# Small steps of the folded maxima with one operand in PSUM, and five key blocks by keys in the last attention

## The chip, the cores and the metric

The kernel runs on one core of a Trainium2 chip. The metric is device time in microseconds of one execution, median of several runs. TensorE (PE) multiplies matrices into PSUM, VectorE (DVE) and ScalarE (ACT) work on SBUF and PSUM, GpSimd (POOL) works on SBUF, and SyncE (SP) issues the loads and stores.

## What is computed

Two attention layers follow each other, on two images of 1024 positions and 256 channels. Of the reference this matters:

```
xn = group_norm(x, gamma, beta)            # 32 groups
q, k, v = conv1x1(xn, wq, bq), conv1x1(xn, wk, bk), conv1x1(xn, wv, bv)
scores = einsum('bnc,bmc->bnm', q, k) * C ** -0.5
attn = softmax(scores, axis=-1)
out = conv1x1(einsum('bnm,bmc->bnc', attn, v), wp, bp) + x
```

The second layer does the same with its own weights on the output of the first.

## The kernel before

**Units and chunks.** A unit `u` (0 to 3) is one image in one layer: units 0 and 1 are the images in layer one, 2 and 3 in layer two. A unit has 1024 queries, handled as two chunks of 512, so there are eight chunks `c` from 0 to 7; chunk `2u` is called `first` and chunk `2u + 1` `second` in the code. A chunk has eight key blocks `kb` of 128 keys and four query blocks `j` of 128 queries.

**One chunk.** PE makes the scores of a key block, 128 keys by 512 queries, in one of six PSUM banks (`ring`) with six matmuls (L1027 to L1029). ACT copies them to `S` in SBUF (L449), and DVE keeps a running maximum over the key blocks in `R` (L673). When all eight blocks are in, the maximum over the 128 partitions of `R` must be had for each query and stand on all partitions. For chunks 0 and 1 PE does this with transposes. For chunks 2 to 7 DVE does it alone in `maxima_to_all` (L689 to L721): a transpose of 32x32 squares into the PSUM bank `X`, a reduction of `X` to `folded` (128x16), then eight small steps on 64 or 32 partitions and 16 columns that fold the four groups of 32 partitions into one minimum of the negated values, subtract and add the query's own value `w_query`, and write `spread`; a last transpose spreads it over the whole bank `X`. Each of these steps waits for the one before it by the semaphore `dv_fold`. Then DVE adds `X` to each block of `S` (`shifted`, L729), ACT takes the exponential twice (L456 to `P_hi`, L457 back to `S`), and POOL makes `P_lo`, the difference of the two (L312). The attention of a chunk multiplies `P_hi` and `P_lo` with the values `V` (`attend`, L1066 to L1068, three matmuls for a query block and a key block, accumulated in one bank for each query block). DVE divides by the row sum and adds to `xnat` (`output`, L735 and L739), and in layer two SP stores the rows (L279).

**Order.** Every engine's order is written out by hand, and semaphores are counted. On PE the order in a unit is: values of the unit (`values`, L1013 to L1015), scores of `first`, attention of the chunk before, scores of `second`, attention of `first`, and between its second and third query block the product `t` for the next unit's first half. `values` and `scores` use banks of the ring in turn; a bank is free when DVE has read it, so `values(u, 6)` waits for DVE's `v_low(u, 0)` (L662, L664), which itself follows ACT's `v_high(u, 0)` (L442). While DVE does `maxima_to_all(second)` in units 1 and 2, POOL does `x_low` for the next unit, four subtractions of 128x512 in SBUF (L336). In the first score block of the second half PE also transposes rows of `xnat` for the next unit (`next_rows`, L914), which waits for DVE's `output`.

**The end.** The attention of the last chunk has nothing behind it to hide it. Its first four key blocks are multiplied as they come (`attention_by_keys`: for one `kb`, all four query blocks, behind a wait for that block's `P_lo`). Then one wait asks for `P_lo` of all eight blocks, and the other four are done query block by query block (L1162), so that each query block can be divided and stored while the next is multiplied.

The functions that the change touches follow, and what calls them.

Of the kernel before, what the change touches and what calls it, by code (L numbers as in the profile page):

```python
# [7 lines left out]
ALU = mybir.AluOpType  # L8
# [3 lines left out]
P = 128  # L12
# [7 lines left out]
def two_attention_layers(nc, x, layers, vectors, out):  # L20
# [17 lines left out]
    NB = N // P  # L38
# [3 lines left out]
    SQ = 32  # L42
    BLOCKS = BANK // SQ
    QUARTERS = P // SQ
    BY_PE = 2
    W_COPIES = 2 * QUARTERS
    PER_GROUP = C // GROUPS
    WX = C + 2
# [14 lines left out]
    def tile_of(c, kb):  # L63

        return (c * NB + kb) % TILES
# [28 lines left out]
    with ExitStack() as ctx:  # L94
        def sb(name, shape, dt=F32, stack=ctx):
            return stack.enter_context(nc.sbuf_tensor(name, shape, dt))

        def ps(name):
            return ctx.enter_context(nc.psum_tensor(name, [P, BANK], F32))

        def sem(name):
            return ctx.enter_context(nc.semaphore(name))
# [23 lines left out]
        neg_less = sb("neg_less", [P, QB])  # L126
        neg_shift = sb("neg_shift", [P, QB])
        folded = sb("folded", [P, 2, BLOCKS])
        other = sb("other", [2 * SQ, 2, BLOCKS])
        w_query = sb("w_query", [2 * SQ, HALVES, BLOCKS])  # L130
        spread = sb("spread", [P, BLOCKS])
        S = sb("S", [P, TILES, BANK])
# [31 lines left out]
        X = ps("X")  # L164
# [60 lines left out]
        dv_fold = sem("dv_fold")  # L225
        dv_X = sem("dv_X")
# [9 lines left out]
        def count_R(c, kb):  # L236

            return c * (NB - 1) + kb
# [45 lines left out]
        def _(pool):  # L284
# [30 lines left out]
            def values_of_queries(u):  # L315
# [5 lines left out]
                pool.wait_ge(po_resid, (u + 1) * NB)  # L321
                for n in range(W_COPIES):
                    g, to = divmod(n, 2)

                    if n:
                        pool.wait_ge(po_w, (u - 1) * W_COPIES + n)
                    nc.gpsimd.tensor_copy(by_group[to * SQ:(to + 1) * SQ, g],
                                          w_row[g * SQ:(g + 1) * SQ, :].rearrange("p (h j) -> p h j", j=QB)
                                          ).then_inc(po_w, 1)
                pool.wait_ge(po_w, u * W_COPIES)  # L330

# [198 lines left out]
        def _(dve):  # L530
# [158 lines left out]
            def maxima_to_all(c):  # L689

                half, quarter, n = 2 * SQ, SQ, c - BY_PE
                dve.wait_ge(dv_R, count_R(c, NB - 1))
                nc.vector.transpose(X[:], R[:]).then_inc(dv_fold, 1)
                dve.wait_ge(dv_fold, 7 * n + 1)
                nc.vector.tensor_reduce(folded[:, 0, :], X[:, :].rearrange("p (b n) -> p b n", n=SQ), AX_X, ALU.max,
                                        negate=True).then_inc(dv_fold, 1)  # L700
                dve.wait_ge(dv_fold, 7 * n + 2)
                nc.vector.tensor_copy(other[0:half, 0, :], folded[half:P, 0, :]).then_inc(dv_fold, 1)
                dve.wait_ge(dv_fold, 7 * n + 3)
                nc.vector.tensor_tensor(folded[0:half, 1, :], folded[0:half, 0, :], other[0:half, 0, :], ALU.min
                                        ).then_inc(dv_fold, 1)
                dve.wait_ge(dv_fold, 7 * n + 4)
                nc.vector.tensor_copy(other[0:quarter, 1, :], folded[quarter:half, 1, :])
                nc.vector.tensor_copy(other[quarter:half, 1, :], folded[0:quarter, 1, :]).then_inc(dv_fold, 1)
                dve.wait_ge(dv_fold, 7 * n + 5)
                nc.vector.tensor_tensor(other[0:half, 0, :], folded[0:half, 1, :], other[0:half, 1, :], ALU.min  # L710
                                        ).then_inc(dv_fold, 1)

                w = w_query[:, c % 2, :]
                dve.wait_ge(po_w, c // 2 * W_COPIES)
                dve.wait_ge(dv_fold, 7 * n + 6)
                nc.vector.tensor_tensor(folded[0:half, 1, :], other[0:half, 0, :], w, ALU.subtract).then_inc(dv_fold, 1)
                dve.wait_ge(dv_fold, 7 * n + 7)
                nc.vector.tensor_tensor(spread[0:half, :], folded[0:half, 1, :], w, ALU.add)
                nc.vector.tensor_tensor(spread[half:P, :], folded[0:half, 1, :], w, ALU.add).then_inc(dv_X, 1)
                dve.wait_ge(dv_X, 2 * n + 1)  # L720
                nc.vector.transpose(X[:], spread[:, :, None].to_broadcast([P, BLOCKS, SQ])).then_inc(dv_X, 1)  # L721

            def shifted(c, kb):
                if c < BY_PE:
                    dve.wait_ge(pe_M, c + 1)
                else:
                    dve.wait_ge(dv_X, 2 * (c - BY_PE) + 2)
                tile = S[:, tile_of(c, kb), :]
                nc.vector.tensor_tensor(tile, X[:], tile, ALU.add).then_inc(dv_D, 1)  # L729
# [63 lines left out]
            for u in range(1, UNITS):  # L793
# [8 lines left out]
                for kb in range(1, NB):  # L802
                    running_max(first, kb)
                    if more and kb in (3, 6):
                        statistics_of(u + 1, kb // 3 - 1)

                maxima_to_all(first)
                output(before, 0)
                for kb in range(4):
# [32 lines left out]
                running_max(second, 7)  # L842

                maxima_to_all(second)
                output(first, 0)
                shifted(second, 0)
# [24 lines left out]
        def _(pe):  # L871
# [191 lines left out]
            def attend(c, j, kb):  # L1063
                v, tile, mine = V[(c // 2) % 2], exp_of(c, kb), slice(j * P, (j + 1) * P)
                bank = bank_of("O", c, j)
                nc.tensor.matmul(bank[:, 0:C + 2], P_hi[:, tile, mine], v[:, kb, 0:C + 2], start=(kb == 0), stop=False)  # L1066
                nc.tensor.matmul(bank[:, 0:C], P_hi[:, tile, mine], v[:, kb, C + 2:VX], start=False, stop=False)  # L1067
                last = nc.tensor.matmul(bank[:, 0:C + 2], P_lo[:, tile, mine], v[:, kb, 0:C + 2],  # L1068
                                        start=False, stop=(kb == NB - 1))
                if kb == NB - 1:  # L1070
                    last.then_inc(pe_O, 1)
# [13 lines left out]
            def attention_by_keys(c, kb):  # L1085

                pe.wait_ge(po_P, c * NB + kb + 1)
                for j in range(QB):
                    if kb == 0:
                        wait_for_bank("O", c, j)  # L1090
                    attend(c, j, kb)
# [64 lines left out]

                attention(first, next_first_half, lambda: None)

            for kb in range(NB // 2):
                attention_by_keys(CHUNKS - 1, kb)  # L1160
            pe.wait_ge(po_P, CHUNKS * NB)
            for j in range(QB):  # L1162
                for kb in range(NB // 2, NB):
                    attend(CHUNKS - 1, j, kb)


# [30 lines left out]
```

## Time and profile before

| | us |
|---|---|
| median of 3 runs | 264.69 |
| range of the runs | 264.43 to 264.79 |
| the profiled execution, whole | 264.73 |
| its span, first to last instruction | 262.6 |

The busy times in the profiled execution are PE 254.3 us, DVE 187.5, ACT 153.3 and POOL 124.2. The granted TensorE clock is 1.0 in all 40 slices of the span. PE's busy time hides short gaps, since the end of a matmul is modelled: where it matters, read the starts of two neighbouring rows. Matmuls of 256 or 258 columns start 0.12 us apart when nothing holds them, those of 512 columns 0.23 us apart.

### The profile page before, as it was taken

How to read it: one execution, taken by the hardware profiler on the slowest of the kernel's cores; microseconds unless marked ns; L12 is line 12 of the kernel's file. 1: busy time of each engine (PE TensorE's matmuls, PEld its weight loads, DVE VectorE, ACT ScalarE, POOL GpSimd, SP SyncE). 2: the span in 40 equal slices, each digit the busy share in tenths (PEclk: the TensorE clock that was granted, in tenths of full speed). 3: DMA queues.
4: the chain of work that ended last, by engine and by line, in shares of the span. 5: the costliest groups of instructions: out<-in, count | busy, mean ns of one | idle time of the engine just before them, and what ended most of it. 6: DMA issues, size and time to landing. Idle time of an engine off the chain costs nothing.

```text
span 262.6 us, 4590 instructions
## 1 busy us (share of the span) xinstructions
PE 254.3 (97%) x1614; PEld 228.2 (87%) x1614; DVE 187.5 (71%) x473; ACT 153.3 (58%) x299; POOL 124.2 (47%) x143
## 2 busy tenths in 40 slices
PE   7999999999999999999989999999999999999985
PEld 6787789889998899789987899789987899889985
DVE  0589977886983797679776698679776688549703
ACT  3656544699984519645667509746486509740920
POOL 2010801285769209517475907717274917800860
PEclk9999999999999999999999999999999999999999
DMA  6960000000000000000000000000110001100102
GB/s 201 347 217 0 0 1 2 0 0 2 0 4 0 0 2 1 0 2 1 0 1 2 0 2 0 0 2 0 41 41 3 0 2 40 40 2 19 50 14 80
DMA packets 6989, 7.37 MB, mean 28 GB/s; under 512 B 556, under 2 KB 6712, under 8 KB 6968
## 3 DMA queue, kind: packets, MB, share of 16 engines
q1 hardware_dynamic: 6944, 7.08, 8.1%
q8 instruction: 13, 0.21, 0.4%
q14 instruction: 8, 0.07, 0.1%
q10 hardware_dynamic: 24, 0.01, 0.0%
HBM read 4.99 MB, written 2.10 MB: 27 GB/s over the span
## 4 chain that ended last, share of the span: by engine, by line
PE 60%; DVE 21%; ACT 8%; issue 6%; POOL 4%; POOLq 0%; DVEq 0%; ACTq 0%
PE ring L1027 11%; PE ring L1029 10%; PE ring L1028 10%; PE ring L1066 5%; PE ring L1068 4%; PE ring L1067 4%; DVE S L729 4%; POOL P_lo L312 3%; ACT P_hi L456 3%; DVE xnat L739 2%; PE ring L1013 2%; ACT S L457 2%; PE ring L1014 2%; PE ring L1015 2%; PE Z L914 2%
## 5 line engine op out<-in xcount | busy, mean ns | idle before, releaser
L312 POOL TENSOR_TENSOR P_lo<-S,P_hi 128x512 fp32r<-128x512 f32 x64 | 81.9, 1302 | 73.7 <-ACT S L457 73.5
L1066 PE MATMUL ring<-V,P_hi 128*128 128x258 f32 x256 | 72.9, 285 | 0.9 <-POOL P_lo L312 0.9
L1068 PE MATMUL ring<-V,P_lo 128*128 128x258 f32 x256 | 72.2, 282 | 0.0
L1067 PE MATMUL ring<-V,P_hi 128*128 128x256 f32 x256 | 72.2, 282 | 0.0
L456 ACT ACTIVATE P_hi<-S 128x512 fp32r<-128x512 f32 x64 | 40.2, 628 | 43.0 <-DVE S L729 43.0
L449 ACT COPY S<-ring 128x512 f32<-128x512 f32 x64 | 37.2, 589 | 37.9 <-PE ring L1029 36.2
L1027 PE MATMUL ring<-t_hi,xn_lo 128*128 128x512 f32 x128 | 51.8, 405 | 0.0
L1029 PE MATMUL ring<-t_hi,xn_hi 128*128 128x512 f32 x128 | 50.0, 391 | 0.0
L1028 PE MATMUL ring<-t_lo,xn_hi 128*128 128x512 f32 x128 | 50.0, 391 | 0.0
L1066 PEld LDWEIGHTS ring<-V,P_hi 128*128 128x128 f32 x256 | 48.4, 189 | 1.6 <-POOL P_lo L312 1.1
L1067 PEld LDWEIGHTS ring<-V,P_hi 128*128 128x128 f32 x256 | 48.4, 189 | 0.5
L1068 PEld LDWEIGHTS ring<-V,P_lo 128*128 128x128 f32 x256 | 48.6, 190 | 0.0
L673 DVE TENSOR_TENSOR R<-ring,R 128x512 f32<-128x512 f32 x48 | 33.1, 691 | 20.0 <-ACT S L449 19.6
L729 DVE TENSOR_TENSOR S<-X,S 128x512 f32<-128x512 f32 x64 | 41.4, 681 | 1.2 <-PE X L1059 1.2
L457 ACT ACTIVATE S<-S 128x512 f32<-128x512 f32 x64 | 39.8, 622 | 0.0
L308 POOL TENSOR_TENSOR xnat<-xnat,out_bias 128x256 f32<-128x256 f32 x32 | 23.0, 750 | 12.2 <-DVE out_bias L573 12.2
L1027 PEld LDWEIGHTS ring<-t_hi,xn_lo 128*128 128x128 f32 x128 | 24.1, 188 | 5.2 <-issue 0.8
L1029 PEld LDWEIGHTS ring<-t_hi,xn_hi 128*128 128x128 f32 x128 | 24.0, 188 | 5.2
L1028 PEld LDWEIGHTS ring<-t_lo,xn_hi 128*128 128x128 f32 x128 | 24.1, 188 | 4.2
L1013 PE MATMUL ring<-Wx_hi,xn_lo 128*128 128x258 f32 x64 | 18.7, 292 | 1.6 <-DVE w_row L664 1.5
L662 DVE TENSOR_TENSOR V<-ring,V 128x256 fp32r<-128x256 f32 x32 | 13.4, 419 | 9.0 <-ACT V L442 8.9
L1014 PE MATMUL ring<-Wx_lo,xn_hi 128*128 128x258 f32 x64 | 18.2, 284 | 0.0
(116 smaller groups left out, 355.4 us busy)
## 6 DMA issues: line engine op xcount, KB each, us to landing
xnat<-in_x SPq DMA_DIRECT2D x8, 256.0 KB, 6.9
out<-xnat SPq DMA_DIRECT2D x16, 128.0 KB, 1.7
wide<-in_vectors SPq DMA_DIRECT2D x2, 384.0 KB, 7.6
w_wq<-in_L_conv_wq SPq DMA_DIRECT2D x2, 256.0 KB, 4.8
w_wk<-in_L_conv_wk SPq DMA_DIRECT2D x2, 256.0 KB, 5.0
w_wv<-in_L_conv_wv SPq DMA_DIRECT2D x2, 256.0 KB, 6.9
w_wp<-in_L_conv_wp SPq DMA_DIRECT2D x1, 256.0 KB, 6.6
w_wp<-in_L_conv_wo SPq DMA_DIRECT2D x1, 256.0 KB, 7.5
```

What stands on the lines that cost most here:

```text
L312: nc.gpsimd.tensor_tensor(P_lo[:, exp_of(c, kb), :], S[:, tile_of(c, kb), :], P_hi[:, exp_of(c, kb), :].bitcast(F32), ALU.subtract).then_i ...
L449: nc.scalar.copy(S[:, tile_of(c, kb), :], bank_of("S", c, kb)[:]).then_inc(ac_S, 1)
L456: nc.scalar.activation(P_hi[:, exp_of(c, kb), :], S[:, tile, :], ACT.Exp)
L457: nc.scalar.activation(S[:, tile, :], S[:, tile, :], ACT.Exp).then_inc(ac_P, 1)
L673: nc.vector.tensor_tensor(R[:], bank_of("S", c, kb)[:], earlier, ALU.max).then_inc(dv_R, 1)
L729: nc.vector.tensor_tensor(tile, X[:], tile, ALU.add).then_inc(dv_D, 1)
L1027: nc.tensor.matmul(bank[:], xn_lo[:, kc, keys], t_hi[:, kc, cols], start=(kc == 0), stop=False)
L1028: nc.tensor.matmul(bank[:], xn_hi[:, kc, keys], t_lo[:, kc, cols], start=False, stop=False)
L1029: last = nc.tensor.matmul(bank[:], xn_hi[:, kc, keys], t_hi[:, kc, cols], start=False, stop=(kc == KC - 1))
L1066: nc.tensor.matmul(bank[:, 0:C + 2], P_hi[:, tile, mine], v[:, kb, 0:C + 2], start=(kb == 0), stop=False)
L1067: nc.tensor.matmul(bank[:, 0:C], P_hi[:, tile, mine], v[:, kb, C + 2:VX], start=False, stop=False)
L1068: last = nc.tensor.matmul(bank[:, 0:C + 2], P_lo[:, tile, mine], v[:, kb, 0:C + 2], start=False, stop=(kb == NB - 1))
```

## The change

**One.** The buffer `other` in SBUF is gone. The small steps of `maxima_to_all` keep their number, order, sizes and waits, but four groups of 16 columns at the front of the bank `X`, which the reduction before them has finished reading, take the place of `other` and of the second half of `folded` where needed, so that every step has one operand (a source or the destination) in PSUM and none has two sources in SBUF.

**Two.** In the last attention five key blocks instead of four are done by keys, and three instead of four by query block, behind the wait for all `P_lo`.

```diff
+    BY_KEYS = 5
...
-        other = sb("other", [2 * SQ, 2, BLOCKS])
...
-                nc.vector.tensor_copy(other[0:half, 0, :], folded[half:P, 0, :]).then_inc(dv_fold, 1)
+
+                at = [X[:, BLOCKS * m:BLOCKS * (m + 1)] for m in range(4)]
+                nc.vector.tensor_copy(at[0][0:half], folded[half:P, 0, :]).then_inc(dv_fold, 1)
                 dve.wait_ge(dv_fold, 7 * n + 3)
-                nc.vector.tensor_tensor(folded[0:half, 1, :], folded[0:half, 0, :], other[0:half, 0, :], ALU.min
+                nc.vector.tensor_tensor(folded[0:half, 1, :], at[0][0:half], folded[0:half, 0, :], ALU.min
                                         ).then_inc(dv_fold, 1)
                 dve.wait_ge(dv_fold, 7 * n + 4)
-                nc.vector.tensor_copy(other[0:quarter, 1, :], folded[quarter:half, 1, :])
-                nc.vector.tensor_copy(other[quarter:half, 1, :], folded[0:quarter, 1, :]).then_inc(dv_fold, 1)
+                nc.vector.tensor_copy(at[1][0:quarter], folded[quarter:half, 1, :])
+                nc.vector.tensor_copy(at[1][quarter:half], folded[0:quarter, 1, :]).then_inc(dv_fold, 1)
                 dve.wait_ge(dv_fold, 7 * n + 5)
-                nc.vector.tensor_tensor(other[0:half, 0, :], folded[0:half, 1, :], other[0:half, 1, :], ALU.min
+                nc.vector.tensor_tensor(at[2][0:half], at[1][0:half], folded[0:half, 1, :], ALU.min
...
-                nc.vector.tensor_tensor(folded[0:half, 1, :], other[0:half, 0, :], w, ALU.subtract).then_inc(dv_fold, 1)
+                nc.vector.tensor_tensor(at[3][0:half], at[2][0:half], w, ALU.subtract).then_inc(dv_fold, 1)
                 dve.wait_ge(dv_fold, 7 * n + 7)
-                nc.vector.tensor_tensor(spread[0:half, :], folded[0:half, 1, :], w, ALU.add)
-                nc.vector.tensor_tensor(spread[half:P, :], folded[0:half, 1, :], w, ALU.add).then_inc(dv_X, 1)
+                nc.vector.tensor_tensor(spread[0:half, :], at[3][0:half], w, ALU.add)
+                nc.vector.tensor_tensor(spread[half:P, :], at[3][0:half], w, ALU.add).then_inc(dv_X, 1)
...
-            for kb in range(NB // 2):
+            for kb in range(BY_KEYS):
                 attention_by_keys(CHUNKS - 1, kb)
             pe.wait_ge(po_P, CHUNKS * NB)
             for j in range(QB):
-                for kb in range(NB // 2, NB):
+                for kb in range(BY_KEYS, NB):
                     attend(CHUNKS - 1, j, kb)
```

On DVE, in each of the six calls of `maxima_to_all`, this stood in a row before, between the reduction of `X` and the last transpose:

```order
L699 TENSOR_REDUCE folded<-X 128x16 [waits dv_fold]
L702 COPY other<-folded 64x16 [waits dv_fold]
L704 TENSOR_TENSOR folded<-folded,other 64x16 [waits dv_fold]
L707 COPY other<-folded 32x16 [waits dv_fold]
L708 COPY other<-folded 32x16
L710 TENSOR_TENSOR other<-folded,other 64x16 [waits dv_fold]
L716 TENSOR_TENSOR folded<-other,w_query 64x16 [waits dv_fold,po_w]
L718 TENSOR_TENSOR spread<-folded,w_query 64x16 [waits dv_fold]
L719 TENSOR_TENSOR spread<-folded,w_query 64x16
```

At the same place on DVE there stands now:

```order
L699 TENSOR_REDUCE folded<-X 128x16 [waits dv_fold]
L704 COPY X<-folded 64x16 [waits dv_fold]
L706 TENSOR_TENSOR folded<-X,folded 64x16 [waits dv_fold]
L709 COPY X<-folded 32x16 [waits dv_fold]
L710 COPY X<-folded 32x16
L712 TENSOR_TENSOR X<-X,folded 64x16 [waits dv_fold]
L718 TENSOR_TENSOR X<-X,w_query 64x16 [waits dv_fold,po_w]
L720 TENSOR_TENSOR spread<-X,w_query 64x16 [waits dv_fold]
L721 TENSOR_TENSOR spread<-X,w_query 64x16
```

Nothing moved here; only the operands differ, five steps read `X` and five write it.

On PE, in the attention of the last chunk (ring2 to ring5 are the banks of its four query blocks), this stood before around the wait for all of `P_lo`, which is the wait in these rows:

```order
L1068 MATMUL ring5<-V1,P_lo 128x258
L1066 MATMUL ring2<-V1,P_hi 128x258 [waits po_P]
L1067 MATMUL ring2<-V1,P_hi 128x256
L1068 MATMUL ring2<-V1,P_lo 128x258
L1066 MATMUL ring2<-V1,P_hi 128x258
```

At the same place in PE's order this stands now; the first wait is for the fifth block alone, the second for all:

```order
L1070 MATMUL ring5<-V1,P_lo 128x258
L1068 MATMUL ring2<-V1,P_hi 128x258 [waits po_P]
L1069 MATMUL ring2<-V1,P_hi 128x256
L1070 MATMUL ring2<-V1,P_lo 128x258
L1068 MATMUL ring3<-V1,P_hi 128x258
...
L1070 MATMUL ring5<-V1,P_lo 128x258
L1068 MATMUL ring2<-V1,P_hi 128x258 [waits po_P]
```

The wait for all of `P_lo` has moved twelve matmuls later; its former place waits only for the fifth block, and the stretch on one bank behind it is nine matmuls long instead of twelve.

## Rows read from the trace of the kernel before

**Rows 1.** The page, engines: busy us (share of the span) and instructions.

```profile
PE 254.3 (97%) x1614; PEld 228.2 (87%) x1614; DVE 187.5 (71%) x473; ACT 153.3 (58%) x299; POOL 124.2 (47%) x143
```

**Rows 2.** Waits of the whole span: us in total, times, longest.

```profile
PE ring L1013 <- DVE w_row L664: 1.5, 2, 0.8
...
PE ring L1066 <- POOL P_lo L312: 0.9, 1, 0.9
```

**Rows 3.** Busy by stretch, chunks 2, 3: length, PE, PEld, DVE, ACT, POOL, clock, DMA.

```profile
93.40:95.10 1.70, 1.70 (x17) 1.70 (x16) 1.38 (x9) 0.00 (x0) 0.00 (x0) 1.00 0.00 0
120.40:124.95 4.55, 4.55 (x33) 4.22 (x32) 4.23 (x9) 1.32 (x3) 3.48 (x3) 1.00 0.00 0
```

**Rows 4.** Timeline of DVE in chunk 3's `maxima_to_all`: start us, us, line, out<-in.

```profile
118.99 0.73 DVE L697 STREAM_TRANSPOSE X<-R 128x512 f32<-128x512 f32 x1
...
120.48 0.93 DVE L702 COPY other<-folded 64x16 f32<-64x16 f32 x1
121.45 1.21 DVE L704 TENSOR_TENSOR folded<-folded,other 64x16 f32<-64x16 f32 x1
122.69 1.21 DVE L707 COPY other<-folded 32x16 f32<-32x16 f32 x1
```

**Rows 5.** Timeline of POOL in the same stretch, four instructions in one row.

```profile
118.83 5.05 POOL L336 TENSOR_TENSOR xn_lo<-xraw,xn_hi 128x512 fp32r<-128x512 f32 x4 [4.45 <-ACT xn_hi L411]
```

**Rows 6.** Groups of DVE by form: busy us, mean ns of one, idle before.

```profile
L697 DVE STREAM_TRANSPOSE X<-R 128x512 f32<-128x512 f32 x6 | 4.4, 727 | 0.2
...
L699 DVE TENSOR_REDUCE folded<-X 128x16 f32<-128x512 f32 x6 | 4.2, 692 | 0.2
...
L589 DVE TENSOR_TENSOR dev<-dev 128x2 f32<-128x2 f32 x4 | 0.6, 160 | 0.1
...
L585 DVE COPY gmean<-Z 128x2 f32<-128x2 f32 x4 | 0.6, 152 | 0.8 <-PE Z L921 0.8
```

**Rows 7.** Timeline of the last attention, PE and then POOL.

```profile
252.56 0.28 PE L1068 MATMUL ring<-V,P_lo 128*128 128x258 f32 x1
253.71 0.39 PE L1066 MATMUL ring<-V,P_hi 128*128 128x258 f32 x1 [0.87 <-POOL P_lo L312]
253.94 0.28 PE L1067 MATMUL ring<-V,P_hi 128*128 128x256 f32 x1
...
243.59 10.06 POOL L312 TENSOR_TENSOR P_lo<-S,P_hi 128x512 fp32r<-128x512 f32 x8 [14.88 <-ACT S L457]
```

**Rows 8.** Timeline of DVE beside that POOL row.

```profile
244.65 2.47 DVE L729 TENSOR_TENSOR S<-X,S 128x512 f32<-128x512 f32 x4
```

**Rows 9.** Timeline of ACT and DVE from chunk 3's exponentials to unit 2's values.

```profile
127.18 0.63 ACT L456 ACTIVATE P_hi<-S 128x512 fp32r<-128x512 f32 x1 [5.46 <-DVE S L729]
...
135.81 0.90 ACT L442 CAST V<-ring 128x256 fp32r<-128x256 f32 x3
...
136.19 0.43 DVE L662 TENSOR_TENSOR V<-ring,V 128x256 fp32r<-128x256 f32 x1 [1.31 <-ACT V L442]
```

**Rows 10.** Timeline of PE at the values and first scores, units 2 and 3.

```profile
135.84 0.28 PE L1015 MATMUL ring<-Wx_hi,xn_hi 128*128 128x258 f32 x1
136.79 0.39 PE L1013 MATMUL ring<-Wx_hi,xn_lo 128*128 128x258 f32 x1 [0.67 <-DVE w_row L664]
...
139.63 0.40 PE L1029 MATMUL ring<-t_hi,xn_hi 128*128 128x512 f32 x1
140.03 0.48 PE L1027 MATMUL ring<-t_hi,xn_lo 128*128 128x512 f32 x1
...
196.18 0.28 PE L1015 MATMUL ring<-Wx_hi,xn_hi 128*128 128x258 f32 x1
197.29 0.39 PE L1013 MATMUL ring<-Wx_hi,xn_lo 128*128 128x258 f32 x1 [0.83 <-DVE w_row L664]
```

**Rows 11.** Timeline of PE in unit 2's second scores, where rows are transposed.

```profile
167.09 0.63 PE L914 MATMUL Z<-ident,xnat 128*128 128x128 f32 x4 [0.26 <-DVE xnat L739]
```

**Rows 12.** The page, DMA issues: count, KB each, median us to landing.

```profile
out<-xnat SPq DMA_DIRECT2D x16, 128.0 KB, 1.7
```

## The prediction

> **What bounds the kernel now.** I read the shares first: PE is busy for 97% of the span, the next engine for 71% [rows 1]. So the time is PE's work plus the moments in which PE stands still, and an engine beside it matters only where PE waits for it. The grouped waits name two such places that the change can reach [rows 2]: PE waits twice, 1.5 us in all, for DVE's `w_row` before a `values` block, and once, 0.9 us, for POOL's `P_lo` in the last attention. Both edits aim at one of these.
>
> Where does DVE lose time ahead of the first? The stretches of the small steps tell: in chunk 2 they fill 1.70 us with POOL idle, in chunk 3 they take 4.55 us with POOL busy for 3.48 of it [rows 3]. The six calls fall in two kinds: chunks 2, 4, 6 and 7 are like the first row, chunks 3 and 5 like the second. In chunk 3 the copy, the minimum and the next copy took 0.93, 1.21 and 1.21 us [rows 4], against 0.17 for each in chunk 2 (nine rows share 1.38 us busy there [rows 3]). POOL's row holds four subtractions in 5.05 us from 118.83 [rows 5], one each 1.26 us, so they should end at about 120.1, 121.4, 122.6 and 123.9. The slow steps end at 121.41, 122.66 and 123.90: each ends with a POOL instruction. A DVE step whose operands all lie in SBUF stands until the POOL instruction then running is through. The transpose `X<-R`, source in SBUF and destination in PSUM, ran beside the same POOL row in its usual time, 0.73 [rows 4] against a mean of 727 ns [rows 6]. So did four `S<-X,S`, one source in PSUM and one in SBUF, 2.47 us beside a POOL row that fills 243.6 to 253.65 [rows 7, 8].
>
> **Part one, the small steps.** In chunks 3 and 5 the stretch should shrink from 4.55 to 1.70, so 2.85 us each on DVE. That is not yet time of the kernel. What follows on DVE, ACT and POOL moves up until something else comes last. ACT had been idle for 5.46 us before chunk 3's first exponential [rows 9], so it can start 2.85 earlier; its `v_high` of unit 2 began at 135.81 behind those exponentials and DVE's `v_low` at 136.19 behind that [rows 9]. PE stood from 135.96 (135.84 and one slot of 0.12) to 136.79: 0.83, and its next slot was 0.11 too long while it restarted, 0.94 in all [rows 10]. DVE must therefore be 0.83 earlier and has 2.85 to give. Some of it is lost where DVE meets `output` of chunk 2's last query block, whose matmuls end only when the values begin; this is worth about 0.6, which leaves `w_row` some 2.2 us earlier than it was, and the stall goes whole. In unit 3 it is 197.29 - 196.18 - 0.12 = 0.99 and 0.11, together 1.10.
>
> Right behind, at the first two score blocks, PE waits for the banks that the same late `v_low` empties: 140.03 - 139.63 - 0.23 = 0.17 [rows 10], a smaller step one block before and a slow restart behind each, by the starts of the rows 0.35 in all, and it is the same in unit 3. The middle thus gives 0.94 + 0.35 = 1.29 and 1.10 + 0.35 = 1.45, or **2.75 us**. If the followers stay, it is 2.05.
>
> What do the steps cost that had no POOL beside them? No row shows a small copy into PSUM. A transpose that writes PSUM took 727 ns for 512 columns, a reduction that reads PSUM and writes SBUF 692; a two-column copy out of PSUM took 152 and a two-column step within SBUF 160 [rows 6]. Five of the eight steps now read PSUM and five write it, so a call changes by between 5 x -8 = -0.04 and 5 x 35 = +0.18 us. Four calls had no cover from POOL. In chunk 7 there is 0.45 us of room (below), in chunk 6 no PE wait follows. In chunks 2 and 4 the chain runs on to `output` and to PE's transposes of rows in the second half, where PE waits 0.26 us by its row [rows 11]; that place is exposed, in units 1 and 2. So 2 x (-0.04 to +0.18), that is -0.1 to +0.4. I take 0, since reading, where the rows compare small steps with small steps, costs nothing; the 35 ns come from a 512-column transpose, a different thing.
>
> These rows show no dearer read from PSUM. The Trainium skill ("VectorE: DVE Perf Modes", the section on the TRN2 errata) gives a copy from PSUM a fixed cost of 120 cycles against 58 from SBUF at 0.96 GHz. By that rule five reads would add an estimated 0.32 us to a call and 0.65 us over the two exposed places, and the result would be 261.5; the trace disagrees, with 152 against 160 ns, so this changes nothing in the sum.
>
> **Part two, five blocks by keys.** PE's last matmul of the four blocks starts at 252.56, the next could start at 252.68. It starts at 253.71, when POOL's eighth subtraction has ended at 253.65, and its second at 253.94 where 252.80 was possible [rows 7]: **1.14 us** lost. Now twelve matmuls of the fifth block stand there; POOL's row puts their `P_lo` at 243.59 + 5 x 1.26 = 249.9, long there. They take 12 x 0.12 = 1.43 us, to 254.11, and by then all of `P_lo` has been there for 0.45 us. The work is the same, so PE ends 1.14 earlier. The query blocks now end 9 x 0.12 = 1.08 us apart instead of 1.43. DVE needs about 0.9 for one `output`, which still fits. A store lands 1.7 us after its issue [rows 12], so two overlap; what a store loses to the one before it I put at 0 to 0.2 us and take 0.
>
> **Sum.** 2.75 + 1.14 = 3.9 us. The profiled execution took 264.73, the median of the runs is 264.69; both give **260.8**.
>
> **The rivals.**
>
> *Copies into PSUM still wait for POOL.* If it is the copy's source in SBUF that matters, the first copy ends at 121.41 as before, the minimum passes, the second copy waits to 122.65 and the third, now first behind it, to 123.9: the same end as before, and the middle gives nothing. Only 1.14 is left: 263.6. For it: the only row of SBUF to PSUM is a transpose. Against it: that transpose did not wait [rows 4].
>
> No row shows a copy with one end in PSUM beside POOL. The Trainium skill ("SBUF — State Buffer", the section on who interferes with whom) lets a copy contend with GpSimd only in a mode that needs source and destination in SBUF; by it this rival falls, and the result is 260.8.
>
> *Another wait takes the place.* DVE comes to `output` of chunk 2's third block only 0.4 us after PE has it, and the fourth is late by 0.6. If more such meetings eat half of the 2.85, `w_row` comes just in time and the followers stay, or a part of the stall: half of the 2.75 is lost, 262.2.
>
> *Slower than before: every small step on PSUM is dear.* Let a step cost d more. Chunks 2 and 4 expose 16 d; chunk 7 delays `P_lo` and with it PE's last wait by 8 d - 0.45; in chunks 3 and 5 the gain holds up to about 8 d = 2. The cost 24 d - 0.45 passes the gain of 3.9 from d = 0.18, that is when a step takes 0.35 instead of 0.17. At 0.25 it is 5.55, or 266.4. For it: nothing shows small writes to PSUM. Against it: the largest difference in the rows is 0.035 for a whole bank [rows 6].
>
> **How the numbers follow.** My forecast has 0.80 (its own range 260.4 to 261.5: followers 0.7 up, exposed steps -0.1 to +0.4, store 0.2, not all at once), the substituted wait 0.09, the copies 0.07, the dear steps 0.04. About 0.5 us, 0.2%, is what a measurement can tell from no change. The range is 260.3 to 262.0: it holds the forecast's ends with a little of the second rival. Faster by over 0.2% are the first three cases, 0.96; the dear steps split into 0.01 within and 0.03 slower.
>
> **What would show it.** In the changed profile all six calls should fill about 1.7 us between reduction and last transpose, with POOL's four subtractions still beside two of them; a step over 0.3 us in chunks 3 or 5 means that a copy still waits. The waits of PE for `w_row` before L1013 should be gone from the list, and no start of PE be more than 0.03 late at the first two score blocks of units 2 and 3. In the last attention PE should run without a gap, with POOL's last subtraction ending 0.4 us before the wait. The wait before L914 should stay at 0.2 to 0.3; if it grows to 0.6, the steps on PSUM are dear. I am wrong if PE's starts become slower while nobody makes it wait, since my sum has no such term.

## The result

The changed kernel takes 260.69 us, median of 5 runs (260.44 to 261.13), against 264.69 us for the kernel before (264.43 to 264.87, 5 runs). The ratio is 0.9852 with a 95% interval of 0.9839 to 0.9864. The forecast was 260.8, with a range of 260.3 to 262.0.

The engines' row of the page of the changed kernel answers to [rows 1]:

```profile
span 259.0 us, 4590 instructions
...
PE 253.2 (98%) x1614; PEld 228.3 (88%) x1614; DVE 182.2 (70%) x473; ACT 153.7 (59%) x299; POOL 124.2 (48%) x143
```

DVE has lost 5.3 us of busy time, PE 1.1, and the span is 3.6 us shorter. DVE lost more than the kernel did, because only what PE had waited for counts. So the waits of PE over the whole span are the place to look (us in total, times, longest). They answer to [rows 2]:

```profile
PE Z L916 <- DVE xnat L741: 0.5, 2, 0.3
...
PE ring L1002 <- DVE xn_lo L627: 0.2, 1, 0.2
```

Both waits of [rows 2], for `w_row` and for `P_lo`, are no longer in the list. The wait for `xnat` ahead of the transposes of rows, in [rows 11] 0.26, now has 0.21 and 0.27, in units 1 and 2.

The small steps by stretch, chunks 2 and 3 (columns as in [rows 3]):

```profile
93.80:95.50 1.70, 1.70 (x17) 1.70 (x15) 1.40 (x9) 0.00 (x0) 0.00 (x0) 1.00 0.00 0
120.85:122.55 1.70, 1.70 (x17) 1.70 (x16) 1.40 (x9) 1.32 (x3) 1.70 (x2) 1.00 0.00 0
```

Chunk 3 now needs the same 1.70 us as chunk 2, with POOL busy for all of it. The single steps there, on DVE, and POOL beside them:

```profile
119.44 0.73 DVE L697 STREAM_TRANSPOSE X<-R 128x512 f32<-128x512 f32 x1
...
120.93 0.17 DVE L704 COPY X<-folded 64x16 f32<-64x16 f32 x1
121.14 0.17 DVE L706 TENSOR_TENSOR folded<-X,folded 64x16 f32<-64x16 f32 x1
121.34 0.17 DVE L709 COPY X<-folded 32x16 f32<-32x16 f32 x1
121.52 0.17 DVE L710 COPY X<-folded 32x16 f32<-32x16 f32 x1
...
122.00 0.17 DVE L718 TENSOR_TENSOR X<-X,w_query 64x16 f32<-64x16 f32 x1
122.21 0.17 DVE L720 TENSOR_TENSOR spread<-X,w_query 64x16 f32<-64x16 f32 x1
122.39 0.17 DVE L721 TENSOR_TENSOR spread<-X,w_query 64x16 f32<-64x16 f32 x1
122.59 0.73 DVE L723 STREAM_TRANSPOSE X<-spread 128x512 f32<-128x512 f32 x1
...
119.28 5.04 POOL L336 TENSOR_TENSOR xn_lo<-xraw,xn_hi 128x512 fp32r<-128x512 f32 x4 [4.45 <-ACT xn_hi L411]
```

The copy, the minimum and the copy that took 0.93, 1.21 and 1.21 us in [rows 4] take 0.17 each. POOL's row is as long as in [rows 5]: it was never POOL that was held up.

In the last attention PE has no gap left at the place of [rows 7]. These are the starts around the wait for all `P_lo`, the last matmul of the kernel, and POOL's subtractions:

```profile
251.42 0.29 PE L1069 MATMUL ring<-V,P_hi 128*128 128x256 f32 x1
251.54 0.28 PE L1070 MATMUL ring<-V,P_lo 128*128 128x258 f32 x1
251.66 0.28 PE L1068 MATMUL ring<-V,P_hi 128*128 128x258 f32 x1
...
255.84 0.28 PE L1070 MATMUL ring<-V,P_lo 128*128 128x258 f32 x1
...
241.17 10.08 POOL L312 TENSOR_TENSOR P_lo<-S,P_hi 128x512 fp32r<-128x512 f32 x8 [14.84 <-ACT S L457]
```

The row at 251.66 is the first behind the wait for all `P_lo`. POOL's last subtraction ends at 241.17 + 10.08 = 251.25, so 0.41 us of room is left there.

**A measure with less noise.** The head of the kernel, up to the first matmul of the product `t`, depends on when the loads land; it took 18.70 us in the profiled execution before and 19.12 in the one after, and what follows PE's last start took 3.19 in both. So for a few tenths I compare the *body*, from the start of the first of those matmuls to the start of the last matmul. Before it is 259.43 - 18.70 = 240.73 us, after 255.84 - 19.12 = 236.72: **4.01 us** less, which is what the medians say (4.00). The two spans differ by only 3.6 because the head of the profiled execution after was 0.42 longer. The body of the unchanged parts repeats from trace to trace within 0.1 us.

By parts of the body, from the starts of PE's rows: from the first matmul of the values to the first transpose behind the scores, unit 2 took 11.22 us before and takes 9.87 (1.35 less); values and the eight score blocks of unit 3 took 18.20 and take 16.68 (1.52 less); the attentions of chunks 6 and 7, the last of the kernel, took 23.99 together and take 22.86 (1.13 less).

### The profile page after: what moved, and what is told of

The parts are those of the page before. It is cut to its first block, busy times and chain, and to the rows that moved or that the text cites. A ratio compares the mean times of both kernels' runs of the same rounds, so it can differ in the third digit from the quotient of the medians.

```text
span 259.0 us, 4590 instructions
## 1 busy us (share of the span) xinstructions
PE 253.2 (98%) x1614; PEld 228.3 (88%) x1614; DVE 182.2 (70%) x473; ACT 153.7 (59%) x299; POOL 124.2 (48%) x143
## 4 chain that ended last, share of the span: by engine, by line
PE 78%; DVE 11%; issue 5%; ACT 4%; POOL 0%; DVEq 0%; ACTq 0%; POOLq 0%
PE ring L1029 11%; PE ring L1030 11%; PE ring L1031 11%; PE ring L1068 9%; PE ring L1070 9%; PE ring L1069 9%; PE ring L1015 3%; PE ring L1016 3%; PE ring L1017 3%; PE Z L916 2%; PE ring L1002 2%; PE ring L1003 2%; PE ring L1004 2%; DVE S L731 1%; DVE xnat L741 1%
```

## The experiments

Ten kernels were run. `Body` is the measure above; that of the changed kernel is 236.72.

| run | median us | ratio to before (95%) | body |
|---|---|---|---|
| before | 264.7 to 265.0 | | 240.73 |
| changed kernel | 260.69 | 0.9852 (0.9839 to 0.9864) | 236.72 |
| e1, steps only | 262.30 | 0.9925 (0.9899 to 0.9952) | 237.94 |
| e2, keys only | 263.60 | 0.9957 (0.9944 to 0.9970) | 239.62 |
| e3, output first | 260.23 | 0.9832 (0.9819 to 0.9845) | 236.11 |
| e4, six by keys | 260.97 | 0.9864 (0.9841 to 0.9887) | 236.78 |
| e5, last three in SBUF | 262.29 | 0.9929 (0.9888 to 0.9971) | 238.01 |
| e6, one copy more | 261.07 | 0.9860 (0.9829 to 0.9891) | 237.10 |
| e7, two copies more | 261.36 | 0.9868 (0.9853 to 0.9883) | 237.47 |
| e8, longer in 2 and 4 | 261.28 | 0.9868 (0.9850 to 0.9887) | 237.33 |
| e9, longer in 6 | 260.75 | 0.9841 (0.9795 to 0.9887) | 236.74 |
| e10, longer in 7 | 260.54 | 0.9829 (0.9778 to 0.9879) | 236.80 |

### One part alone: e1 and e2

e1 is the changed kernel with the old last attention:

```diff
-    BY_KEYS = 5
+    BY_KEYS = 4
```

> Only the small steps of the maxima on PSUM; the last attention has four key blocks by keys as before. Theory: the stalls of PE before the values of units 2 and 3 and their followers go (2.87 us by the starts of PE's rows in the changed kernel), the wait for the last P_lo stays at 1.1 us. 264.7 - 2.9 = 261.8 us. Rival: the two parts share a cause, PE coming earlier to the last attention waits longer there for P_lo, and the steps alone give less than 2, over 262.7.

e2 is the kernel before with the new last attention:

```diff
-            for kb in range(NB // 2):
+            for kb in range(BY_KEYS):
                 attention_by_keys(CHUNKS - 1, kb)
             pe.wait_ge(po_P, CHUNKS * NB)
             for j in range(QB):
-                for kb in range(NB // 2, NB):
+                for kb in range(BY_KEYS, NB):
```

> Only the fifth key block by keys; the small steps stay within SBUF as before. Theory: 1.14 us at the last attention and nothing else, 263.6 us, both stalls of PE for w_row (0.8 and 1.0) still there. Rival that the parts are not independent: 262.8 or less, or 264.3 or more.

e2 gave 263.60, as expected, and its body is 1.11 us shorter than before. e1 gave 262.30, half a microsecond above its forecast of 261.8, but its body is 2.79 shorter. The median carries what the head did in each of the four executions (264.27, 262.48, 262.13 and 262.11), and only the profiled one, 264.27, shows its head: it began its first `t` matmul only at 21.04 us. There PE had waited for a load:

```profile
PE ring L916 <- DMA xnat<-in_x: 1.5, 1, 1.5
...
PE ring L1068 <- POOL P_lo L312: 0.9, 1, 0.9
PE Z L916 <- DVE xnat L741: 0.5, 2, 0.3
```

(waits of PE in e1), and the granted TensorE clock of its first 21 us, by the view of busy time by stretch, was 0.92 on average instead of 1.00. How much of the 0.5 us the heads of the other three hold is not shown. The second row is the wait that the fifth block removes, back at 0.9. In e2 the other wait is there, in full:

```profile
PE ring L1014 <- DVE w_row L665: 1.5, 2, 0.8
```

The bodies add up: 2.79 + 1.11 = 3.90 of the 4.01 for both. The rival, one part eating the other's gain, falls: PE's arrival at the last attention and the arrival of `P_lo` both hang on the scores of chunk 7, so a shift in the middle moves both.

### Which step waits for POOL: e5, e6 and e7

In e5 the first five small steps stay on PSUM and the last three go back to SBUF:

```diff
-                nc.vector.tensor_tensor(at[2][0:half], at[1][0:half], folded[0:half, 1, :], ALU.min
+                nc.vector.tensor_tensor(other[0:half], at[1][0:half], folded[0:half, 1, :], ALU.min
...
-                nc.vector.tensor_tensor(at[3][0:half], at[2][0:half], w, ALU.subtract).then_inc(dv_fold, 1)
+                nc.vector.tensor_tensor(folded[0:half, 1, :], other[0:half], w, ALU.subtract).then_inc(dv_fold, 1)
...
-                nc.vector.tensor_tensor(spread[0:half, :], at[3][0:half], w, ALU.add)
-                nc.vector.tensor_tensor(spread[half:P, :], at[3][0:half], w, ALU.add).then_inc(dv_X, 1)
+                nc.vector.tensor_tensor(spread[0:half, :], folded[0:half, 1, :], w, ALU.add)
+                nc.vector.tensor_tensor(spread[half:P, :], folded[0:half, 1, :], w, ALU.add).then_inc(dv_X, 1)
```

> The changed kernel, but the last three small steps (subtract and two adds of the query's value) have both sources in SBUF again, as before; the first five keep their operand in PSUM. Theory: in chunks 3 and 5 the steps now come 2.8 us earlier than they did before, so POOL's third and fourth subtraction run beside them, and the wait moves to them: the subtract ends with POOL's third, about 1.1 us, the first add with its fourth, 1.2 us, the last add 0.17. The calls take 3.6 us instead of 1.66, 0.9 remains of the 2.8 us, PE's stalls for w_row nearly go and their followers stay: 0.7 to 0.9 us more than the changed kernel, 261.5 us. Rival: only the copies and minima of the first five steps could meet POOL (as they did in the trace of before, where the last three took 0.17 us): all steps 0.17 us, 260.7 us.

The timeline of DVE in chunk 3 of e5, and POOL's row:

```profile
121.60 0.17 DVE L713 TENSOR_TENSOR other<-X,folded 64x16 f32<-64x16 f32 x1
121.87 1.12 DVE L719 TENSOR_TENSOR folded<-other,w_query 64x16 f32<-64x16 f32 x1
123.02 1.21 DVE L721 TENSOR_TENSOR spread<-folded,w_query 64x16 f32<-64x16 f32 x1
124.25 0.17 DVE L722 TENSOR_TENSOR spread<-folded,w_query 64x16 f32<-64x16 f32 x1
...
119.15 5.05 POOL L337 TENSOR_TENSOR xn_lo<-xraw,xn_hi 128x512 fp32r<-128x512 f32 x4 [4.45 <-ACT xn_hi L412]
```

The subtract and the first add took 0.17 us in the kernel before, because POOL had finished when they came. Now that they come earlier they take 1.12 and 1.21 and end at 122.99 and 124.23, again at POOL's boundaries, and the add behind POOL's end passes at once. So converting some of the steps only moves the wait to the next ones; the change works because no step is left with both sources in SBUF. The call takes 3.64 us from the first copy to the last transpose, against 1.66 in the changed kernel and 4.49 before, so 0.85 is left of the 2.83 us. This is also a measurement of what PE needed, which the prediction put at 0.83 in unit 2 and 0.99 in unit 3. In unit 2, where PE needed 0.83, the stall before the values is gone with 0.85 and only its followers remain; in unit 3, where it needed 0.99, a small one is back:

```profile
195.62 0.28 PE L1018 MATMUL ring<-Wx_hi,xn_hi 128*128 128x258 f32 x1
196.01 0.39 PE L1016 MATMUL ring<-Wx_hi,xn_lo 128*128 128x258 f32 x1
```

0.39 instead of 0.12 between two starts. The body is 1.29 us longer than the changed kernel's; unit 2 has 0.48 of it and unit 3 0.74. The forecast of 0.7 to 0.9 was too low: it counted the followers, 0.35 in each unit, and next to nothing for the stall in unit 3, where the slot is 0.27 too long and the next one 0.10. The median, 262.29, has a wide interval.

e6 adds two steps behind the first copy of every call, and e7 two copies; nothing reads what they write:

```diff
+                nc.vector.tensor_reduce(spare[0:half, 0, 0:1], folded[0:half, 0, :], AX_X, ALU.max)
+                nc.vector.tensor_copy(spare[0:half, 1, :], folded[0:half, 0, :])
```

> The changed kernel with two more instructions behind the first copy of each call, whose results nobody reads: a reduction of 64x16 in SBUF to 64x1 in SBUF, and a copy of 64x16 within SBUF. Theory that the way of reading counts and not the place alone: the reduction takes under 0.2 us in all six calls, the copy stands in chunks 3 and 5 until POOL's running subtraction ends, 0.4 to 1.3 us. Rival that any step wholly within SBUF waits: the reduction is the one that stands. Theory on time: DVE loses 0.8 to 1.5 us in chunks 3 and 5 of the 2.8 it gained and PE needs 0.8 to 1.0, so no stall before the values comes back; in chunks 2 and 4 two steps of 0.17 to 0.2 us are exposed, 0.7 us together: 261.3 to 261.5 us.

```diff
+                nc.vector.tensor_copy(spare[0:half, 1, :], folded[0:half, 0, :])
+                nc.vector.tensor_copy(spare[0:half, 2, :], folded[0:half, 0, :])
```

> The changed kernel with two more copies of 64x16 within SBUF behind the first copy of each call, whose results nobody reads. Theory: in chunks 3 and 5 each stands until a POOL subtraction ends, together 1.5 to 2.5 us, of 2.8 gained; 0.3 to 1.3 us are left, about what PE needs, so the stall of w_row comes back by up to 0.5 us and the waits behind it (0.35 to 0.5 a unit) too; with 0.7 us exposed in chunks 2 and 4 that is 262.0 to 262.6 us. Rival that the order of the whole 2.8 us counts on PE: 260.7 + 0.7 + two times 2, over 264.

DVE in chunk 3 of e6:

```profile
120.82 0.17 DVE L705 COPY X<-folded 64x16 f32<-64x16 f32 x1
121.02 0.16 DVE L706 TENSOR_REDUCE spare<-folded 64x1 f32<-64x16 f32 x1
121.11 0.64 DVE L707 COPY spare<-folded 64x16 f32<-64x16 f32 x1
121.67 0.16 DVE L709 TENSOR_TENSOR folded<-X,folded 64x16 f32<-64x16 f32 x1
```

All four read 64x16 of `folded` in SBUF while POOL works, the last three the very same elements, the first the other 64 partitions. The copy into PSUM passes in 0.17, the reduction within SBUF in 0.16, the copy within SBUF stands for 0.64 until POOL's boundary, the minimum with one source in PSUM passes. So it is neither the place of the source nor SBUF as such. In these rows a copy waits when both of its ends are in SBUF, a two-source step when both sources are (e5); a one-source reduction does not wait, though all of its operands are in SBUF. "SBUF — State Buffer" of the Trainium skill, in the section on who interferes with whom, names just these cases (a copy in a two-port mode, a step with two SBUF inputs, never a reduction), and this trace agrees with 0.64, 1.12 and 0.16 us. That the copy here ran in such a mode no run shows.

e7 shows what happens at the boundary, in chunk 3 and then in chunk 5:

```profile
121.01 0.73 DVE L706 COPY spare<-folded 64x16 f32<-64x16 f32 x1
121.66 1.33 DVE L707 COPY spare<-folded 64x16 f32<-64x16 f32 x1
...
180.51 0.72 DVE L706 COPY spare<-folded 64x16 f32<-64x16 f32 x1
181.15 0.16 DVE L707 COPY spare<-folded 64x16 f32<-64x16 f32 x1
```

The same pair of copies: in chunk 3 the second waits for another POOL instruction, in chunk 5 it slips through. A step that follows directly behind one that waited may or may not come before POOL's next; by the profile the second copy starts at 121.66 and 181.15, and POOL's next subtraction at 121.67 and 181.17, too near to tell the two cases apart. The prices on time were forecast too high in both runs, 261.07 where 261.3 to 261.5 was expected and 261.36 where 262.0 to 262.6 was: the two steps more make a call without POOL 0.15 us longer (1.81 instead of 1.66) and not 0.35, so the exposed part in chunks 2 and 4 is smaller, and in e7 only chunk 3 lost two boundaries. In e6 the loss in chunk 3 (2.30 us from the first copy to the last transpose instead of 1.66) brought no stall back before the values, as the theory said, and in e7 the followers came back in unit 2 (0.35 us), while nothing over 0.1 came back in unit 3. The rival that all of DVE's 2.8 us counts falls.

### Which calls are exposed: e8, e9 and e10

Each adds four copies from SBUF to PSUM behind the first copy, in some calls alone: in e8 for chunks 2 and 4, as in this diff, in e9 for chunk 6, in e10 for chunk 7. Nothing reads what they write.

```diff
+                if c in (2, 4):
+                    for m in range(4):
+                        nc.vector.tensor_copy(X[0:half, BLOCKS * (8 + m):BLOCKS * (9 + m)], folded[0:half, 0, :])
```

> The changed kernel with four more copies of 64x16 from SBUF to PSUM, whose results nobody reads, in the calls for chunks 2 and 4 alone. Theory: these calls are exposed in full at PE's transposes of rows in the second scores; four steps of 0.17 to 0.2 us make each wait 0.7 us longer, 1.4 us in all: 262.1 us. Rival: ACT's exponentials or the products for the second half hide it, under 261.3.

> The changed kernel with four more copies of 64x16 from SBUF to PSUM, whose results nobody reads, in the call for chunk 6 alone, 0.7 us. Theory: in unit 3 no rows are transposed for a next unit, so nobody on PE waits for this chain: 260.7 us and no new wait of PE. Rival: the scores of chunk 7 need the product that follows this chain: 261.1 or more.

> The changed kernel with four more copies of 64x16 from SBUF to PSUM, whose results nobody reads, in the call for chunk 7 alone, 0.7 us. Theory: all P_lo come 0.7 us later and had 0.4 us of room before PE asks for all of them: PE waits 0.3 us there, 261.0 us. Rival: PE already waits for single blocks of P_lo at the start of the last attention, or the room is larger: 261.4, or 260.7.

The four copies cost less than forecast. DVE in chunk 2 of e8, and PE's wait for `xnat` over the whole of e8:

```profile
93.23 0.17 DVE L704 COPY X<-folded 64x16 f32<-64x16 f32 x1
93.44 0.40 DVE L707 COPY X<-folded 64x16 f32<-64x16 f32 x4
93.75 0.16 DVE L709 TENSOR_TENSOR folded<-X,folded 64x16 f32<-64x16 f32 x1
...
PE Z L919 <- DVE xnat L744: 1.1, 2, 0.6
```

93.75 - 93.44 = 0.31 us for four, not 0.7, and from its first copy to its last transpose the call takes 1.96 us instead of 1.67, 0.30 more. The two waits of PE rise from 0.5 to 1.1 us in sum, so by 0.6, and the body by 0.61, which is 2 x 0.30: every tenth of a microsecond in these two calls is a tenth of the kernel's time. The median, 261.28, lies at the rival's number (under 261.3), but the waits and the body show the full length of what was added, so nothing hid it: the mechanism stands, and the price of these steps was wrong by a factor of two. In e9 the same 0.30 us in chunk 6 changed the body by 0.02, within its noise, and no wait of PE is new. In e10, in chunk 7, the body changed by 0.08, also within its noise, with no wait for `P_lo` in PE's rows, where the forecast had one of 0.3 us and 261.0: POOL's last subtraction ends at 250.45 and PE asks at 250.59, so 0.14 of the 0.41 us of room is left, and this run does not say what happens beyond it.

### The end: e4

```diff
-    BY_KEYS = 5
+    BY_KEYS = 6
```

> The changed kernel with six key blocks by keys in the last attention and two by query block. Theory: no wait for P_lo is left to remove; the query blocks end 0.72 us apart, DVE needs 0.67 from one reciprocal to the next, so the last output starts at the same time: 260.7 us, at most 0.2 more because stores of 128 KB every 0.72 us meet each other. Rival: DVE or the stores do not keep up at 0.72 us, and the end is 0.4 us or more later, 261.1 or more.

260.97, body 236.78 and 3.18 us behind it: the same as with five (236.72 and 3.19). DVE just keeps up at 0.72 us a query block, with no idle time between two outputs:

```profile
254.25 0.17 DVE L737 RECIPROCAL row_inv<-ring 128x1 f32<-128x1 f32 x1
254.52 0.48 DVE L741 SCALAR_TENSOR_TENSOR xnat<-ring,row_inv,xnat 128x256 f32<-128x256 f32 x1
254.97 0.17 DVE L737 RECIPROCAL row_inv<-ring 128x1 f32<-128x1 f32 x1
```

So five is enough and six gives nothing, as expected. The last four stores landed 1.7 us after their issue, each, with six as with five, although with six up to three of them are under way at a time.

### A better order: e3

What PE still waits for is the output ahead of the transposes of rows. On DVE it stood behind a statistic that nobody needed yet:

```diff
                 output(before, 2)
+                output(before, 3)
                 if more:
                     statistics_of(u + 1, 2)
-                output(before, 3)
```

> The changed kernel, and on DVE in the first halves of units 1 and 2 the output of the fourth query block of the chunk before goes ahead of the statistics of the third pair of row blocks instead of behind them. Theory: PE's transposes of rows in the second scores wait for this output, 0.21 and 0.27 us by the waits, 0.37 and 0.43 against the usual pace; the output comes 0.7 us earlier, both waits go, 0.8 us less: 259.9 us. Rival: the statistics, now 0.7 us later, hold back the mean over groups and with it PE two score blocks on, or the query block is not ready at DVE yet: 260.5 or more.

Both waits are gone from the list of PE, and the transposes of unit 2 start on time, 0.23 behind the matmul ahead of them instead of 0.66:

```profile
164.96 0.40 PE L1031 MATMUL ring<-t_hi,xn_hi 128*128 128x512 f32 x1
165.19 0.60 PE L916 MATMUL Z<-ident,xnat 128*128 128x128 f32 x4
```

The median is 260.23 us, ratio to before 0.9832 (0.9819 to 0.9845); the body is 0.61 shorter than the changed kernel's, the median 0.46. This is the fastest of all. 0.8 was expected; the rival has its share. The two places give 0.86 by PE's starts; around the mean over groups, two score blocks on, whose statistics now come later, PE's slots are 0.08 us longer in each unit, and 0.07 in the score blocks ahead of it in unit 2, so the later statistics are felt a little, as the rival has it.

## Why the prediction was right

The body is 4.01 us shorter where 2.75 + 1.14 = 3.89 was forecast, and each term of the sum is close to what its part of the kernel shows, so the number is no luck of errors that cancel.

**What bounds the kernel.** Right. PE has the same 1614 matmuls, and the parts of the body that got shorter are those where it waited.

**Small steps, chunks 3 and 5.** Right: 2.85 us each was forecast on DVE, 4.49 - 1.66 = 2.83 measured. The cause is shown by e5 and e6, not only by coincident ends. But the rule as it was put, that a step waits when all its operands lie in SBUF, is wider than what the runs show: the reduction within SBUF took 0.16 us beside POOL in e6. For the eight steps here, copies and two-source steps, it makes no difference.

**What of it reaches PE.** 0.94 + 0.35 in unit 2 and 1.10 + 0.35 in unit 3 were forecast, together 2.75; by PE's starts it is 1.35 + 1.52 = 2.87, and 2.79 in e1. Slot by slot against the changed kernel, the two stalls with their restarts give 0.94 and 1.10, as forecast. The followers give 0.39 and 0.38 and not 0.35, the last 0.06 lies in differences of 0.01 or less. One step of the working was wrong without effect: I let DVE lose 0.6 us where it meets the last `output` of chunk 2. It does stand there, 0.48 us, but ACT's cast of the values comes later still, so nothing is lost:

```profile
132.32 0.17 DVE L737 RECIPROCAL row_inv<-ring 128x1 f32<-128x1 f32 x1 [0.48 <-PE ring L1070]
...
133.82 0.43 DVE L662 TENSOR_TENSOR V<-ring,V 128x256 fp32r<-128x256 f32 x1 [0.74 <-ACT V L442]
```

Counted from the first matmul of the values, `w_row` is ready after 2.25 us where it was 5.10: the full 2.85.

**The uncovered calls.** -0.04 to +0.18 us a call was the bound, 0 was taken; the stretch from the first copy to the last transpose went from 1.63 to 1.66 or 1.67 us, up to +0.04. A step that writes PSUM takes 2 to 8 ns more than the same step into SBUF (175 against 167 for the second minimum and the subtract, 173 against 170 for the first copy), one that only reads it the same 167, within 2 ns. The Trainium skill ("VectorE: DVE Perf Modes", the section on the TRN2 errata) gives a read from PSUM 62 cycles more of fixed cost than one from SBUF. That does not appear here either, now with the very same two-source steps side by side; a copy of this size out of PSUM was not run. That both places are exposed one to one was argued; e8 shows it.

**Five blocks by keys.** 1.14 forecast, 1.13 measured (1.11 in e2), with 0.41 us of room for `P_lo` where 0.45 was forecast. The stores cost nothing, as taken. DVE was given 0.9 us for one `output`; e4 shows four in a row 0.72 apart, so it needs no more than that, and the conclusion that it fits into 1.08 holds.

**The rivals.** Copies into PSUM do not wait (0.17 beside POOL); no other wait took the place of the one removed; a step that writes PSUM is 2 to 8 ns dearer, not 180. The signs named in the prediction came: 1.7 us in all six calls, no wait for `w_row`, no gap in the last attention and 0.4 us of room there, and 0.21 and 0.27 before the transposes of rows.

## What to carry to other kernels

A chain of tiny dependent VectorE steps beside long GpSimd instructions pays up to one GpSimd instruction per step, although each step is 0.17 us of work: look for small instructions whose duration is bimodal in the trace and ends with GpSimd's. If a spare corner of a PSUM bank is at hand, give every copy and every two-source step of the chain one operand there, all of them, since half a conversion moves the wait. Value such a saving by the gap on the bounding engine (here 0.8 to 1.0 of 2.83 us, and what follows right behind it, 1.35 and 1.52 in all), and value the last wait of a kernel by asking what work stands behind it that already has its data.

## What the runs showed that was not expected

**Small steps do not all start at the same distance.** In e8 the four extra copies start 0.08 us apart, where steps that wait for each other's semaphore start 0.20 apart. It would be quick to call the difference the price of the semaphore, but the rows do not bear that out. The first of the four copies has no wait either, and it starts 0.2 behind the copy ahead of it (93.44 against 93.23). The second of each pair of half steps, L710 and L721, carries no wait (against what the section on the kernel before says of each step, and as the order rows show), and starts 0.18 behind the first in all six calls of the changed kernel. What these starts have in common is that a source or the destination begins at another partition than in the step before, while the copies 0.08 apart all begin at partition 0. A wait alone goes with the longer distance too: L720 begins at the same partitions as L718, waits for it, and starts 0.21 behind it. So either of the two is enough here, by these rows; no run was made to separate them, and why it is so stays open.

**The boundary.** Of two copies one behind the other across a GpSimd boundary, the second took 1.33 us in one chunk and 0.16 in another of the same execution.

**One such step is left.** In the changed kernel the small subtract of chunk 1 (L685, 128x4, both sources in SBUF) takes 1.16 us and ends within 0.03 us of one of POOL's subtractions, against 0.16 in chunk 0 with POOL idle. It is as long in the kernel before (1.14), and no wait in PE's list names it.
